# A recurrence behind a mixture-of-experts pipeline: a shorter first chunk, and two more PSUM banks for the attention behind the last step

## The reference

```python
x = x + L0(x, cond)     # gated shared network + top-2 of 8 experts
x = x + L1(x, cond)     # the same kind of layer, twice the shared width
x = x + L2(cond, x)     # recurrence over the 256 time steps
x = x + L3(x, cond)     # causal attention, 16 heads of 8, one image key
# L2, one step:
gate  = sigmoid(h @ Wh.T + z_t @ Wz.T + b)
h_new = tanh(h * (1 - alpha) + gate * z_t)
```

## Time and profile before

| what | us |
|---|---|
| median of 3 runs | 525.72 (524.05 to 529.68) |
| the profiled execution, its own time | 526.6 |
| its span, first to last instruction | 524.8 |
| PE busy in the span | 472.7 (90%) |
| DVE busy | 367.1 (70%) |
| ACT busy | 265.1 (51%) |
| POOL busy | 29.3 (6%) |
| mean granted clock of PE | 0.961 of full |

### The profile page before, as it was taken

One profiled execution on the slowest core, in us unless ns is written; L12 is line 12 of the kernel. 1 busy time (PEld: TensorE's weight loads), 2 busy tenths in 40 slices (PEclk: granted clock), 3 DMA queues, 4 the chain that ended last, 5 costly groups with the idle time before them and its releaser, 6 DMA issues.

```text
span 524.8 us, 12683 instructions
## 1 busy us (share of the span) xinstructions
PE 472.7 (90%) x4202; PEld 313.3 (60%) x4202; DVE 367.1 (70%) x1629; ACT 265.1 (51%) x1072; POOL 29.3 (6%) x92
## 2 busy tenths in 40 slices
PE   4898998898998989989998878999997999999995
PEld 2676676566675766757764335566654566666662
DVE  5877888998888888889786688977432855455511
ACT  3432544634555455554455654465659344444472
POOL 7210100000001000010000000000000000000000
PEclk9999898999999998999999868999999799999998
DMA  8400000000000000000000000000000000000000
GB/s 311 182 0 2 2 2 0 2 2 1 2 1 2 2 0 2 2 1 2 1 1 2 1 2 1 2 1 2 17 6 1 21 1 3 2 1 22 1 1 21
DMA packets 4911, 8.30 MB, mean 16 GB/s; under 512 B 496, under 2 KB 3824, under 8 KB 4720
## 3 DMA queue, kind: packets, MB, share of 16 engines
q1 hardware_dynamic: 4416, 7.23, 3.9%
q10 hardware_dynamic: 432, 0.27, 0.2%
HBM read 6.44 MB, written 1.05 MB: 14 GB/s over the span
## 4 chain that ended last, share of the span: by engine, by line
PE 58%; DVE 19%; ACT 15%; issue 6%; DMA 1%; ACTq 0%; DVEq 0%
PE ybk L796 11%; PE hid L942 6%; PE ybk L919 6%; PE cbk L964 5%; DVE vbk L1270 4%; PE hid L897 3%; DVE hlo L1257 3%; PE hid L906 3%; ACT d L708 3%; PE hid L782 2%; PE hid L852 2%; ACT silu L641 2%; ACT hs L721 2%; PE hid L901 2%; ACT hb L648 2%
## 5 line engine op out<-in xcount | busy, mean ns | idle before, releaser
L942 PE MATMUL hid<-xsp,up 128*128 128x256 f16 x672 | 97.1, 286 | 2.1 <-DVE up L1020 1.4
L796 PE MATMUL ybk<-hg,down 128*128 128x256 f32 x352 | 97.0, 399 | 2.2 <-DVE hg L1142 1.4
L708 ACT ACTIVATE d<-cbk 128x8 f32<-128x8 f32 x256 | 45.9, 179 | 95.8 <-PE cbk L964 94.7
L1188 DVE TENSOR_REDUCE wm<-hid 128x2 f32<-128x256 f32 (+2 forms) x107 | 58.8, 554 | 28.6 <-PE hid L855 26.8
L720 ACT ACTIVATE hhi<-vbk 128x8 f16<-128x8 f32 x255 | 45.2, 177 | 62.3 <-DVE vbk L1270 62.1
L1270 DVE TENSOR_TENSOR_SCAN vbk<-d 128x16 f32<-128x16 f32 x256 | 50.5, 197 | 31.3 <-ACT d L708 29.0
L961 PEld LDWEIGHTS cbk<-hhi,wh 128*128 128x128 f16 x512 | 38.5, 100 | 56.1 <-ACT hhi L720 47.3
L698 ACT ACTIVATE hb<-hid,att 128x512 f32<-128x512 f32 x71 | 48.7, 689 | 40.5 <-PE hid L906 40.3
L942 PEld LDWEIGHTS hid<-xsp,up 128*128 128x128 f16 x672 | 61.2, 101 | 12.9 <-issue 1.9
L796 PEld LDWEIGHTS ybk<-hg,down 128*128 128x128 f32 x352 | 60.2, 191 | 8.7 <-DVE hg L1142 2.1
L961 PE MATMUL cbk<-hhi,wh 128*128 128x8 f16 x512 | 51.5, 171 | 13.7 <-ACT hhi L720 12.3
(11 more groups left out here) (166 smaller groups left out, 686.6 us busy)
## 6 DMA issues: line engine op xcount, KB each, us to landing
qz<-up_in SPq DMA_DIRECT2D x3, 512.0 KB, 8.0
kp<-maskr_in SPq DMA_DIRECT2D x1, 1024.0 KB, 12.1
out_dram<-silu SPq DMA_DIRECT2D x4, 256.0 KB, 2.3
x<-x_in SPq DMA_DIRECT2D x7, 128.0 KB, 9.1
down<-down_in SPq DMA_DIRECT2D x1, 768.0 KB, 9.9
att<-att_in SPq DMA_DIRECT2D x1, 751.0 KB, 10.2
down<-down_in SPq DMA_DIRECT2D x1, 640.0 KB, 6.8
qz<-up_in SPq DMA_DIRECT2D x1, 256.0 KB, 4.5
```

The source lines that it names most:

```text
L708: nc.scalar.activation(d1[:, t % 2, :, 0], cbk[c % 2][:, o:o + B], ACT.Tanh, scale=0.5 / RS).then_inc(gate_th, 1)
L796: m = pe.matmul(ybk[l][:, 0:n], D(l, "w2" if shared else "e2", e * f + i), hg[:, hg_of[made] % NHG, i * n:i * n + n], start=first and i == ...
L942: m = pe.matmul(into, up[:, pw, a:a + P], x_part(c, l, px, slice(0, n)), start=j == 0, stop=j == 2)
L1188: i = nc.vector.tensor_reduce(wm[:, b, a * nh + r.start:a * nh + r.stop], hk[:].rearrange("p (h k) -> p h k", h=nh)[:, r], AX.X, ALU.max)
```

## The change

`CHUNKS` becomes two chunks of 16 steps (n = 128 columns, four experts to a bank, so two `E` and two `M` units in a layer) and seven of 32. The x loads follow, one more than before. Behind the last step, the banks that go round are the three, `vbk` and both of `cbk`: six instead of four. Units in one of the latter three wait for the last step, as those in `vbk` did.

```diff
-CHUNKS = (32,) * 8
+CHUNKS = (16, 16) + (32,) * 7
...
+TAIL = 3
...
-    bank_of, before, user, last_use = {}, {}, [None] * (NHT + 1), [0] * (NHT + 1)
+    bank_of, before, user, last_use = {}, {}, [None] * (NHT + TAIL), [0] * (NHT + TAIL)
...
-                at = min(range(NHT + (step == T and phase == "behind")), key=lambda i: last_use[i])
+                at = min(range(NHT + TAIL * (step == T and phase == "behind")), key=lambda i: last_use[i])
...
-        hid = [ps(f"hid{i}") for i in range(NHT)] + [vbk]
+        hid = [ps(f"hid{i}") for i in range(NHT)] + [vbk] + cbk
...
-                if bank_of[key] == NHT:
+                if bank_of[key] >= NHT:
                     pe.wait_ge(h_full, T)
```

## The result

The changed kernel takes 536.9 us (four runs, 536.3 to 537.6) where the kernel before takes 525.9. The ratio is 1.020, 95% interval 1.014 to 1.026: it is slower by 11 us. Forecast were 523.0 us and 512 to 534, so the time lies outside the range and on the other side; rival C, at 0.15, gave 535.0.

A forecast was written before the change was run, and what follows sets the result against it. PE's work list was taken to bound the kernel, not the last step. Short chunks +2.8 us, fewer `AV` runs -3.0 and the hole between blocks -2.5 sum to -2.7: from 525.7 to 523.0 us, range 512 to 534.

The forecast's parts named there:

- rival C: Ahead of step 32: steps stop 18 slots or more, half empty, for chunk 2's two serial routers; 535.0 us, chance 0.15.
- the stage behind the last step: Sign of being right: the attention behind the last step takes 145 to 155 us with PE near full.
- the runs of `AV`: Sign of being right, behind the last step: fewer runs of line 919, some of 16 matmuls.
- PE's wait on the copy of `Q`: Sign of being right, between the attention's blocks: less than 1 us of PE waiting on line 667.
- What bounds the kernel: Whole kernel: it ends when PE has worked off its list; the last step does not set the end.
- Rival A: At the last step: it sets the end, the list behind done as fast as before; 517.7 us, chance 0.10.
- First step at 34.0: Ahead of the first step: chunks of 16 bring it 11.5 us earlier, to 34.0 us, bounds 32 and 38.
- 11.5 us of PE work moved behind: At the first step: PE has done 19.3 us of work instead of 30.8, so 11.5 us moves behind.
- The stop, 9 slots of 0.20 us: Ahead of step 32: steps wait for chunk 2 about 9 slots while PE works on; 1.8 us, bounds 0 and 5.
- The ninth chunk, 1.0: In the step stage: two more router passes load DVE and POOL, about a quarter felt; 1.0 us, 0 to 4.
- Edit 2, -5.5: Behind the last step, six banks instead of four: -3.0 us from fewer `AV` runs, -2.5 us between the blocks.
- The term for the hole: Between the attention's blocks: six banks spare PE the wait for ACT's copy of a `Q` bank; -2.5 us, bounds 0 and -5.

The follow-up runs named there:

- stop18: Kernel before with six banks, chunks all of 32, and step 32 held back until slot 92, a stop of 18 slots: 528.2 us, ratio 1.000.
- x_early: Changed kernel with the attention's preparation behind `C` of chunk 2, and chunk 2 allowed ahead of `C` of chunk 0: 531.4 us, ratio 1.007.
- prep_late: Changed kernel with the attention's preparation allowed only behind `C` of chunk 2 instead of `C` of chunk 1: 530.2 us, ratio 1.004.
- chunks_only: Changed kernel with four banks behind the last step, so the chunks of 16 alone: 541.3 us, ratio 1.026.
- pair_4banks: Kernel before with four banks and only the `AV` units paired, 29 runs of `AV` in block 1 instead of 58: 521.6 us, ratio 0.990.
- pair_qz_dve: Kernel before with six banks, `AV` pairs and all `QZ` of block 1 on DVE instead of half on ACT: 514.1 us, ratio 0.973.
- pair_qz_half: Kernel before with six banks, `AV` pairs, and `QZ` of two head groups on ACT, the rest on DVE: 512.4 us, ratio 0.969.

## Why the prediction was wrong

Of the signs given for being right, the stage behind the last step and the runs of `AV` came as said. The first step (39.7, said 32 to 38), the gap (19.3, said 5 to 14), the last step (386.3, said 368 to 376) and PE's wait on the copy of `Q` (2.3, said under 1) did not.

**What bounds the kernel: right.** PE's list decides, not the last step. stop18 shows it directly: the last step 18 us later, the end 6.4 us later. x_early shows the other half. Rival A falls.

**First step at 34.0: it came at 39.7.** `GT` of layer 0 reached DVE at 19.27, forecast 19.4. The term behind it failed: 16 recorded down-projections stand there, not the 8 that I counted, and PE ran them at the lower level of its clock, behind 3.45 us of idle time (granted clock 0.50 from 18.6 to 25.4 us). Timeline of PE:

```profile
18.97 0.27 PE L762 MATMUL hid<-id,g 128*16 128x128 f16 x1 [3.45 <-DVE lg L1079]
...
21.15 3.72 PE L797 MATMUL ybk<-hg,down 128*128 128x128 f32 x16
25.87 0.22 PE L755 MATMUL hid<-wrx,xsp 128*128 128x8 f16 x3 [1.00 <-DVE xsp L1164]
```

They cost 0.22 us each against 0.12 forecast. Layer 1's router starts at 25.87 instead of 23.0 and takes 6.7 us until `GT` where 6.3 were forecast, and in layer 1 the stretch from `GT` to the start of the step takes 6.9 us (32.57 to 39.44) instead of 4.7 with `C` and the allowance, with chunk 1's down-projections in PE's queue.

**11.5 us of PE work moved behind: right.** Groups of PE ahead of the first step, which answer to the earlier trace rows:

```profile
L943 PE MATMUL hid<-xsp,up 128*128 128x128 f16 x144 | 10.9, 238 | 1.3 <-DVE up L1021 1.3
L797 PE MATMUL ybk<-hg,down 128*128 128x128 f32 x64 | 10.5, 323 | 1.6 <-DVE hg L1143 1.6
L783 PE MATMUL hid<-gt,sel 128*128 128x128 f16 x24 | 2.4, 249 | 1.0 <-DVE hg L1148 0.6 <-DVE gt L1132 0.5
```

144 x 0.055 + 64 x 0.12 + 24 x 0.055 is 16.9 us, with 2.1 for the rest 19.0; forecast were 19.3. So the two terms that were to cancel did not: -6.1 + 11.8 = +5.7 us.

**The stop, 9 slots of 0.20 us: this step failed, and it is the larger part.** It was 16 slots, since I left the attention's preparation out of the list ahead of chunk 2; without it, in prep_late, it is 10. And the preparation left PE empty, which 0.20 us a slot does not cover. That price came from an average over stretches in which two chunks alternate. It held where that was so: prep_late costs 5.7 to 7.9 us over the banks alone, 5.7 are the first stage's, and some 2 at most are left for 10 slots and the ninth chunk. In the changed kernel chunk 2 waited for a router behind the preparation, and the list has no unit for PE in slots 65 to 68. Of the 9.4 us up to the gates, PE needed some 2.4 at full clock: 1.9 for four fp32 matmuls of 512 columns, by twice the 0.24 of the earlier trace rows, and the steps' small ones. That leaves 7 us empty; 4.2 of the 9.4 lie ahead of the stop itself. With 5.7 for the first stage it makes 12.7, where chunks_only shows 14.7 in spans. The other 2 us are not placed. PE has one wait of 1.98 us, up to 69.9, while `IK` holds DVE, which would fit. That the preparation's place is worth 8.1 us is shown by prep_late, and that a stop with full slots is cheap by stop18; the split is worked out.

**The ninth chunk, 1.0: not seen.** From step 32 to 255 the two kernels take 286.0 and 286.1 us, and chunks_only 285.8. No run isolates the term.

**Rival C gave 535.0 near the measured 536.9, in part by luck.** It named a long stop with empty slots, but for two routers in series and not for the preparation; it had the first stage at nothing, where 5.7 us were lost, and the stop at 11 us. Its point of decision was wrong too (slot 88; `C` of chunk 2 came in 84). And the stated range, up to 534, did not take it in.

**Edit 2, -5.5: measured -4.3 to -5.6 by spans, some -3 to -4.6 by medians.** Runs of `AV` in block 1 fell from 58 to 45, forecast 46, at the price forecast. The term for the hole failed: the wait for the bank went from `Q` to `A` (2.3 us on line 668, where less than 1 was given as the sign of being right), and `QZ` on ACT added two more, as the bound of 0 on that term had said. Some 2 us that pair_4banks shows for the banks beside the runs are not placed: `A` in `vbk` and `cbk` comes earlier by the list, but no run isolates it.

## What to carry to other kernels

An earlier start of a serial chain is worth nothing where an engine's list decides the end; count what that engine leaves empty, before and after, and nothing else. Where work is handed out in chunks, a short first chunk takes its time from the second: check that the chunk behind is ready when the short ones are used up, and that no other work (here the attention's preparation) was tied to an event that has moved forward. A stop is cheap when its slots are full (0.2 to 0.35 us each); work that comes too early and leaves the bounding engine empty is dear (8.1 us for six slots).

## What was not expected of the hardware

- PE's clock made part of the loss. With halved matmuls PE was busy 22.4 of 30.3 us ahead of the first step (32.8 of 36.3 before), and it was granted 0.89 of the full clock there (1.00 before) and 0.68 from 76.7 to 86.1; fp32 matmuls of 128 columns then took 0.22 us instead of 0.12. These are stretches at the level of 1.2 GHz within ones at 2.4.
- A lower granted clock lengthened the steps' stage by little. pair_qz_dve and pair_qz_half have the same list up to the last step. From step 32 to 255 the profiled executions take 284.7 us at a granted clock of 0.96 and 289.0 at 0.92, 22.5 and 44.4 us of it at the lower level: an estimate from the two is 0.2 us lost for each us there. The changed kernel had 41 us of it in the same steps and the kernel before 27, at 0.93 and 0.95. All four executions of the changed kernel had a mean of 0.937 to 0.941, so up to 3 us of its loss may be the clock's. What lowered it there was not isolated.
- Entering and leaving a weight tile of 32 columns costs PE 0.18 to 0.29 us each time, with nothing shown as idle for it. Joining neighbours saved 6.2 us of 525 with four banks, where the six banks alone saved 5.6.
